# Two-stage convolution block on one core: a third buffer for half an image, loaded at another place and in quarters

## The chip, the core and the metric

The kernel runs on one core of a Trainium2 chip. The engines named here are TensorE (PE; PEld is its loading of weights), VectorE (DVE), ScalarE (ACT), GpSimd (POOL) and SyncE (SP), which issues all DMAs. The metric is the device time of one execution in microseconds.

## What is computed

`x` is (16, 32, 128, 128) in float32. Two residual steps follow each other:

```python
x = x + L0(_gn(x))      # per-image mixed 3x3 depthwise weights, gate, then 32 -> 32 channels
x = x + L1(_gn(x))
# L1:
hidden = einsum('oc,bchw->bohw', w_hidden, x)            # 32 -> 192 channels
hidden = depthwise 3x3(hidden)                           # SAME padding
q, k, v = split(hidden, 3)                               # 64 channels each
out = irfft2(rfft2(patches(q)) * rfft2(patches(k)))      # 8x8 patches
out_norm = layernorm over the 64 channels(out) * norm_w + norm_b
y = einsum('oc,bchw->bohw', w_out, v * out_norm)         # 64 -> 32 channels
```

`_gn` normalizes each channel over its image.

## The kernel before

The first stage handles image by image: `x` comes in, L0 is computed, and two things are written to memory: `x2_d` (the result of the first residual step, float32) and `xn_d` (the normalized input of L1, split in a high and a low float16 part, with a border of zeros). This takes some 500 us and the change hardly touches it.

The second stage runs over 32 units, each half an image (`u = 2 * image + half`). A unit has a *front* and a *spectral* stretch, and the front of unit u also finishes unit u-1 (its *tail*).

- **Front.** VectorE's `window` (copy L1107) copies one row of patches, 16 patches of 10 x 10 pixels, from the half image `xs` into a buffer `win`; there are 8 rows in a unit and four buffers. TensorE's `hidden_group` (matmuls L568) multiplies a quarter of a row at a time, 32 groups in a unit; ScalarE copies them to `hwin` (L815). Between the groups TensorE computes the v convolution of the tail from the tail's `xs` (`v_chunk`, L587), transposes its normalized pixels (`turn`, L600) and projects (`project`, L609). VectorE computes the tail's statistics (`pixel_stats` L1117, `variance` L1123 and L1125), centres and scales (`centre` L1130, `scale` L1137), gates (`gate` L1142) and adds the residual (`residual` L1149); GpSimd takes the roots (L451).
- **Spectral.** TensorE transforms eight octets of q (L648) and k (L662), VectorE multiplies them (L1201), TensorE goes back (`inverse`, L677, four times), ScalarE moves q (L857) and the result (L870). The last parts of the tail (turn, gate, project, residual) lie in its first third. Four window copies of the next unit stand between the products.

Each engine runs a list written out by hand; what orders them is semaphores. SyncE issues all DMAs. For unit u it waits until the tail's v convolution is done (`s_v_mm`, in `unit_dma`), loads the half image of unit u+1 in four DMAs (`load_xs`, L338: g is one of four copies over 32 partitions each, 536 KB), waits until the tail's four residuals are added, stores them (`store_res`, L391, 4 x 256 KB), waits for this store and loads `res` for unit u (`load_res`, L384, 4 x 256 KB from `x2_d`). There are two `xs` buffers: unit u+1 takes the place of the tail u-1, whose v convolution runs through the whole front of u.

The order in `unit_dma`:

```python
sp.wait_ge(s_v_mm, 8 * u)
if nxt is not None:
    load_xs(*nxt)
sp.wait_ge(s_res_done, 4 * u)
store_res(*prev)
sp.wait_ge(s_out_stored, 64 * u)
if here is not None:
    load_res(*here)
```

A program prints here the functions that the diff touches:

Of the kernel before, what the change touches and what calls it, by code (L numbers as in the profile page):

```python
# [68 lines left out]
def build(nc, t, out):  # L69
# [3 lines left out]
    x = t["x"]  # L73
# [18 lines left out]
    with ctx:  # L92
# [19 lines left out]
        s_xs_in = [semaphore(f"xs_in{s}") for s in range(2)]  # L112
# [128 lines left out]
        dw_t = take(128)  # L241
# [19 lines left out]
        ones_row = take(128)  # L261
        st1, st2 = take(6 * NCH), take(6 * NCH)
# [17 lines left out]
        res = take(2048)  # L280
        top[0] = max(top[0], stage1_end)
        xs = [take(HALF * WP, f16) for _ in range(2)]
        G_q = take(64 * 64)
        G_k = take(64 * 64)
        win = [take(1632, f16) for _ in range(4)]
# [21 lines left out]
        def _(sp):  # L307
# [43 lines left out]
            for b in range(-1, NB + 2):  # L351
# [10 lines left out]
                if b == NB + 1:  # L362
                    load_xs(0, 1)
# [3 lines left out]
                if b == NB - 3:  # L367

                    sp.wait_ge(s_xn_out, 128 * (older + 1))
                    sp.wait_ge(s_pads_stored, 32)  # L370
                    load_xs(0, 0)
# [8 lines left out]
            def load_res(b, half):  # L380
                for jr in range(2):
                    for s in range(2):
                        p0 = 64 * jr + 32 * s
                        sp.dma_start(res[p0:p0 + 32, :].rearrange("p (l r) -> p l r", l=2),  # L384
                                     image_rows(x2_d, b, half, jr, s)).then_inc(s_res_in, 16)

            def store_res(b, half):
                for jr in range(2):
                    for s in range(2):
                        p0 = 64 * jr + 32 * s  # L390
                        sp.dma_start(image_rows(out.rearrange("b c h w -> b c (h w)"), b, half, jr, s),  # L391
                                     res[p0:p0 + 32, :].rearrange("p (l r) -> p l r", l=2)).then_inc(s_out_stored, 16)
# [3 lines left out]

            def unit_dma(u, prev, here, nxt):

                sp.wait_ge(s_v_mm, 8 * u)
                if nxt is not None:  # L400
                    load_xs(*nxt)
                sp.wait_ge(s_res_done, 4 * u)
                store_res(*prev)
                sp.wait_ge(s_out_stored, 64 * u)
                if here is not None:
                    load_res(*here)

            for b in range(NB - 1):
                unit_dma(2 * b + 1, (b, 0), (b, 1), (b + 1, 0))
                unit_dma(2 * b + 2, (b, 1), (b + 1, 0), (b + 1, 1))  # L410
            unit_dma(LAST, (NB - 1, 0), (NB - 1, 1), None)
            unit_dma(LAST + 1, (NB - 1, 1), None, None)
# [4 lines left out]
        def _(pool):  # L417
# [11 lines left out]
            for s in range(4):  # L429
# [3 lines left out]
            pool.wait_ge(s_win_room, 4)  # L433
# [25 lines left out]
        def _(pe):  # L459
# [94 lines left out]
            def hidden_group(u, g, ring):  # L554
# [9 lines left out]
                w = win[g // 4 % 4]  # L564
# [7 lines left out]
            def v_chunk(u, half, k, jr, groups, between):  # L572
# [10 lines left out]
                for tap in range(9):  # L583
                    dy, dx = tap // 3, tap % 3
                    for s in range(2):
                        row = 8 * (2 * s + jr) + dy
                        mm = pe.matmul(v_banks[chunk % 3][64 * s:64 * s + 64, :], v_w[:, 64 * tap:64 * tap + 64],  # L587
                                       at(xs[half], row * WP + 32 * k + dx, [32 * WP, 2], [WP, 8], [1, 32]),
# [23 lines left out]
            def front(u, half, tail):  # L612
# [14 lines left out]
                v_half = 1 - half  # L627
                hidden(3)
                for k in range(4):
                    v_chunk(tail, v_half, k, 1, (5, 5, 4, 3)[k], hidden)  # L630
# [3 lines left out]
                    if k < 3:  # L634
                        v_chunk(tail, v_half, k + 1, 0, (5, 4, 3)[k], hidden)
# [3 lines left out]
            def spectral(u, half, tail):  # L639
# [57 lines left out]
                v_chunk(u, half, 0, 0, 0, None)  # L697

            front(0, 0, None)
            spectral(0, 0, None)  # L700
            for b in range(NB - 1):
                for half in (1, 0):
                    u = 2 * b + 2 - half
                    front(u, half, u - 1)
                    spectral(u, half, u - 1)
            front(LAST, 1, LAST - 1)
            spectral(LAST, 1, LAST - 1)
            front(None, 0, LAST)
# [179 lines left out]
        def _(dve):  # L888
# [212 lines left out]
            def window(u, half, r, b=None):  # L1101

                if positive(32 * u + 4 * (r - 3)):
                    dve.wait_ge(s_hidden_mm, 32 * u + 4 * (r - 3))
                if r == 0:
                    dve.wait_ge(s_xs_in[half], 64 * (b + 1))
                dve.tensor_copy(win[r % 4][:, 0:16 * WIN].rearrange("p (j y x) -> p j y x", y=10, x=10),  # L1107
                                     at(xs[half], 8 * r * WP, [8, 16], [WP, 10], [1, 10])).then_inc(s_win_ready, 1)
# [42 lines left out]
            def front(u, half, tail):  # L1151
                rows = iter(range(4, 8) if u is not None else ())

                def windows(n=1):
                    for r in islice(rows, n):
                        window(u, half, r)

                if tail is None:
# [6 lines left out]
                    windows(3)  # L1165
# [26 lines left out]
            def spectral(u, tail, nxt):  # L1192
# [74 lines left out]
```

## Time and profile before

| | us |
|---|---|
| median of 3 runs | 2653.68 (2650.85 to 2656.28) |
| profiled execution | 2649.98, its span 2648.2 |
| TensorE busy, over the span (48,375 matmuls, as many weight loads) | 2332.2 (88%) |
| VectorE busy | 1610.3 (61%) |
| ScalarE busy | 1453.6 (55%) |
| mean granted TensorE clock | 0.945 of full speed |

Times in the trace count from the span's start. The first unit's front starts at 501.6, unit 1's at 561.3, unit 11's at 1220.6, the last one's (unit 31) at 2548.1. A row of the timeline merges neighbouring instructions of one line; in square brackets stands the engine's idle time before it and what ended it. "issue" there means that the engine waited for nothing that the profile shows. Matmuls are pipelined, so the next group starts before the last one's modelled end.

### The profile page before, as it was taken

The numbers are of one execution on the slowest core, as the hardware profiler recorded it, in microseconds if no ns is written. First come the engines' busy times: TensorE is split into PE (matmuls) and PEld (weight loads), VectorE is DVE, ScalarE is ACT, GpSimd is POOL, SyncE is SP. The second block draws the span as 40 slices with busy tenths as digits, with TensorE's granted clock in tenths as the row PEclk, the third lists the DMA queues.
The fourth block names the chain that finished last, engine by engine and source line by source line (L and its number), as shares of the span: only waits on it lengthen the run. The fifth ranks groups of instructions, "written<-read, shape, count | busy, mean of one in ns | idle before, by whom it ended". The sixth has DMA issues, their size and how long they took to land. (4 is left out here: it accounts for less than half of the span.)

```text
span 2648.2 us, 107033 instructions
## 1 busy us (share of the span) xinstructions
PE 2332.2 (88%) x48375; PEld 1493.1 (56%) x48375; DVE 1610.3 (61%) x4058; ACT 1453.6 (55%) x2629; POOL 476.6 (18%) x324
## 2 busy tenths in 40 slices
PE   7898888698989889898998988989889899998997
PEld 3333333466656566565665666656666566665664
DVE  5667666466656566565665666656666556665565
ACT  3556555655555555555555555555555555555552
POOL 1000000022222222222222222222222222222222
PEclk9899889799999999999999999999999999999999
DMA  6788887723232232222322223222232222322222
GB/s 132 195 234 232 228 219 211 181 71 72 70 72 65 68 73 68 65 62 69 71 70 66 62 69 72 67 67 59 69 74 68 68 52 70 74 68 68 56 51 50
DMA packets 60409, 248.63 MB, mean 94 GB/s; under 512 B 12393, under 2 KB 12658, under 8 KB 53810
## 3 DMA queue, kind: packets, MB, share of 16 engines
q1 hardware_dynamic: 59954, 241.78, 38.0%
q8 instruction: 381, 6.24, 1.0%
q14 instruction: 74, 0.61, 0.1%
HBM read 140.02 MB, written 101.72 MB: 91 GB/s over the span
## 5 line engine op out<-in xcount | busy, mean ns | idle before, releaser
L451 POOL TENSOR_TENSOR arena<-arena 128x8 f32<-128x8 f32 x256 | 452.3, 1767 | 1666.1 <-DVE arena L1123 1661.1
L587 PE MATMUL bank<-arena 128*64 128x512 f16 x4608 | 689.8, 393 | 0.0
L815 ACT ACTIVATE arena<-bank 100x512 f32<-100x512 f32 x1024 | 605.2, 628 | 96.8 <-PE bank L568 75.6
L1201 DVE TENSOR_TENSOR arena<-bank,arena 128x512 f32<-128x512 f32 x512 | 334.7, 685 | 412.9 <-issue 322.8
L568 PEld LDWEIGHTS bank<-arena 128*36 128x36 f16 (+1 forms) x8192 | 330.9, 104 | 232.3 <-issue 25.1
L522 PE MATMUL bank<-arena 32*32 32x508 f32 (+1 forms) x9216 | 377.2, 637 | 50.1 <-issue 35.2
L568 PE MATMUL bank<-arena 128*36 128x128 f16 (+1 forms) x8192 | 389.9, 221 | 17.5 <-DVE arena L1107 9.6
L857 ACT ACTIVATE arena<-bank 128x512 f32<-128x512 f32 x256 | 153.2, 599 | 442.1 <-PE bank L648 440.1
L648 PE MATMUL bank<-arena 100*32 100x128 f32 x8192 | 311.2, 288 | 87.6 <-issue 85.9
L677 PE MATMUL bank<-arena 32*64 32x256 f32 x8192 | 303.0, 417 | 83.6 <-ACT arena L870 46.6
L662 PE MATMUL bank<-arena 100*32 100x128 f32 x8192 | 302.6, 285 | 36.7 <-issue 36.5
L870 ACT ACTIVATE arena<-bank 128x256 f32<-128x256 f32 x512 | 155.2, 390 | 319.2 <-PE bank L677 319.2
L1117 DVE BATCH_NORM_STATS2 arena<-arena 128x6 f32<-128x128 f32 x1024 | 221.7, 279 | 169.2 <-ACT arena L870 169.2
L824 ACT ACTIVATE arena<-bank,arena 128x256 f32<-128x256 f32 x512 | 261.5, 561 | 109.0 <-PE bank L600 108.6
L648 PEld LDWEIGHTS bank<-arena 100*32 100x32 f32 x8192 | 243.6, 115 | 110.7 <-issue 93.4
L662 PEld LDWEIGHTS bank<-arena 100*32 100x32 f32 x8192 | 238.1, 114 | 105.1 <-issue 81.6
L677 PEld LDWEIGHTS bank<-arena 32*64 32x64 f32 x8192 | 194.6, 143 | 166.4 <-issue 135.1
L1142 DVE TENSOR_TENSOR arena<-arena,bank 128x512 f32<-128x512 f32 x256 | 175.3, 685 | 149.4 <-ACT arena L824 149.2
L587 PEld LDWEIGHTS bank<-arena 128*64 128x64 f16 x4608 | 206.1, 109 | 96.1 <-issue 12.4
L522 PEld LDWEIGHTS bank<-arena 32*32 32x32 f32 x9216 | 143.1, 106 | 188.3 <-issue 155.7
L600 PEld LDWEIGHTS bank<-arena 128*128 128x128 f32 x1024 | 133.7, 195 | 107.9 <-DVE arena L1137 76.0
L1137 DVE TENSOR_TENSOR arena<-arena 128x512 f32<-128x512 f32 x256 | 178.1, 696 | 24.8 <-POOL arena L451 0.9
(112 smaller groups left out, 1615.6 us busy)
## 6 DMA issues: line engine op xcount, KB each, us to landing
arena<-xn_d SPq DMA_DIRECT2D x128, 536.2 KB, 8.4
xn_d<-arena SPq DMA_DIRECT2D x130, 260.0 KB, 4.8
x_d<-arena SPq DMA_DIRECT2D x64, 512.0 KB, 8.3
arena<-x_d SPq DMA_DIRECT2D x128, 256.0 KB, 5.0
out<-arena SPq DMA_DIRECT2D x128, 256.0 KB, 4.3
arena<-x_in SPq DMA_DIRECT2D x32, 544.0 KB, 9.8
arena<-x_in SPq DMA_DIRECT2D x32, 528.0 KB, 9.6
arena<-spectra_in SPq DMA_DIRECT2D x1, 384.0 KB
```

Source lines behind the costliest of these rows:

```text
L451: pool.tensor_tensor(tiny["rstd"][:, slot], tiny["var_eps"][:, slot], powers, ALU.pow).then_inc(s_root, 1)
L522: mm = pe.matmul(at(psum_of(t, r)[32 * c:32 * c + 32, :], low, [W, 4], [1, high - low]), conv_w[b % 2][32 * r:32 * r + 32, 32 * tap:32 * t ...
L568: mm = pe.matmul(ring[g % len(ring)][low:high, 128 * i:128 * i + 128], w[:, first + low:first + high], hidden_w, start=True, stop=True)
L587: mm = pe.matmul(v_banks[chunk % 3][64 * s:64 * s + 64, :], v_w[:, 64 * tap:64 * tap + 64], at(xs[half], row * WP + 32 * k + dx, [32 * WP, ...
L648: mm = pe.matmul(q_bank[32 * c:32 * c + 32, first:first + 128], G_q[0:WIN, 64 * ch + 32 * part:64 * ch + 32 * part + 32], hwin[0:WIN, 128 ...
L662: mm = pe.matmul(k_banks[m % 2][32 * c:32 * c + 32, first:first + 128], G_k[0:WIN, 64 * ch + 32 * part:64 * ch + 32 * part + 32], hwin[0:W ...
L677: mm = pe.matmul(i_banks[c][64 * lam:64 * lam + 64, 256 * (e % 2):256 * (e % 2) + 256], small["inverse"][32 * c:32 * c + 32, 64 * both:64 ...
L815: act.activation(h_rows[0:WIN, :, first:first + 4], ring[g % len(ring)][0:WIN, :].rearrange("p (i c) -> p c i", i=4), ACT.Copy).then_inc(s ...
L824: ins = act.activation(at(gated[jr], 256 * lam, [32, 8], [8, 4], [1, 8]), at(banks[4], 64 * lam, [8, 8], [128, 4], [1, 8]), ACT.Identity, ...
L1117: ins = dve.bn_stats(T["pixel_stats"][:, first:first + 6], at(Y, 2048 * s + 4 * p + j, [32, 64], [1, 2]))
L1137: dve.tensor_tensor(piece, piece, over(T["rstd"][:, slot]), ALU.mult).then_inc(s_y_norm, 1)
L1201: dve.tensor_tensor(prod[:, first:first + 512].rearrange("p (a b x) -> p a b x", a=2, b=2), at(k_banks[m % 2], 256 * quad, [128, 2], [0, 2 ...
```

## The change

- There are three `xs` buffers; unit u uses `xs[u % 3]`. The third lies where the first stage has its data, and the small `dw_t` moves among that data to make room.
- `load_xs` for unit u+1 is issued when the first hidden group of unit u is done (`s_hidden_mm` at 32u+1), and after each of its four DMAs SyncE waits for its landing before it issues the next. (The loads of units 0 and 1, in the first stage, stay without such waits.)
- `store_res` waits after each of its four DMAs.
- `load_res` is issued in two halves of two DMAs. The first waits for the third inverse product of unit u, the second for the first half's landing.
- There are three `win` buffers in place of four. Three rows are copied ahead of a unit (in the spectral stretch, after products 8, 10 and 12) in place of four (after 8, 10, 11 and 13); row 3 is now copied in the front, before the first `scale`. The copy of row r waits for 4(r-2) hidden groups of its unit in place of 4(r-3).
- The loops over image and half become one loop over u.

```diff
-            def load_xs(b, half):
+            def load_xs(u, paced=True):
+
+                b, half = divmod(u, 2)
                 for g in range(4):
                     src = xn_d[b, g % 2, :, half * (H // 2):half * (H // 2) + HALF, :].rearrange("c h w -> c (h w)")
-                    sp.dma_start(xs[half][32 * g:32 * g + 32, :], src).then_inc(s_xs_in[half], 16)
+                    sp.dma_start(xs[u % 3][32 * g:32 * g + 32, :], src).then_inc(s_xs_in[u % 3], 16)
+                    if paced:
+                        sp.wait_ge(s_xs_in[u % 3], 64 * (u // 3) + 16 * (g + 1))
...
+            def load_res(u, pair):
+                for s in range(2):
+                    p0 = 64 * pair + 32 * s
+                    sp.dma_start(res[p0:p0 + 32, :].rearrange("p (l r) -> p l r", l=2),
+                                 image_rows(x2_d, u // 2, u % 2, pair, s)).then_inc(s_res_in, 16)
+
+            def store_res(u):
+
+                y = out.rearrange("b c h w -> b c (h w)")
+                sp.wait_ge(s_res_done, 4 * (u + 1))
+                for part in range(4):
+                    pair, s = divmod(part, 2)
+                    sp.dma_start(image_rows(y, u // 2, u % 2, pair, s),
+                                 res[32 * part:32 * part + 32, :].rearrange("p (l r) -> p l r", l=2)).then_inc(s_out_stored, 16)
+                    sp.wait_ge(s_out_stored, 64 * u + 16 * (part + 1))
...
+            load_res(0, 1)
+            for u in range(1, LAST + 1):
+                if u < LAST:
+                    sp.wait_ge(s_hidden_mm, 32 * u + 1)
+                    load_xs(u + 1)
+                store_res(u - 1)
+                sp.wait_ge(s_inverse_mm, 4 * u + 3)
+                load_res(u, 0)
+                sp.wait_ge(s_res_in, 64 * u + 32)
+                load_res(u, 1)
+            store_res(LAST)
...
-                w = win[g // 4 % 4]
+                w = win[(8 * u + g // 4) % 3]
...
-            def window(u, half, r, b=None):
-
-                if positive(32 * u + 4 * (r - 3)):
-                    dve.wait_ge(s_hidden_mm, 32 * u + 4 * (r - 3))
+            def window(u, r):
+
+                if positive(32 * u + 4 * (r - 2)):
+                    dve.wait_ge(s_hidden_mm, 32 * u + 4 * (r - 2))
...
-            def front(u, half, tail):
-                rows = iter(range(4, 8) if u is not None else ())
+            def front(u, tail):
+                rows = iter(range(3, 8) if u is not None else ())
...
                     variance(tail, p)
                     if p == 1:
                         centre(tail, 0)
+                windows()
                 scale(tail, 0)
...
-                    if nxt is not None and n in (8, 10, 11, 13):
-                        window(nxt[0], nxt[1], (8, 10, 11, 13).index(n), nxt[2])
+                    if u < LAST and n in (8, 10, 12):
+                        window(u + 1, n // 2 - 4)
```

## Rows read from the trace of the kernel before

**Rows 1.** Windows, units 1 to 30 (the first line names the columns).

```profile
core 0: us, PE busy (x) PEld busy (x) DVE busy (x) ACT busy (x) POOL busy (x), PEclk, DMA share, GB/s
...
561.30:2548.10 1986.80, 1779.28 (x36482) 1225.34 (x36480) 1204.95 (x3002) 1093.75 (x2160) 424.82 (x240) 0.95 0.29 67
```

**Rows 2.** List of TensorE's waits, units 1 to 30: total us, times, longest us.

```profile
PE bank L648 <- issue: 82.5, 25, 5.4
PE bank L677 <- ACT arena L870: 43.7, 30, 1.5
PE bank L677 <- issue: 36.9, 23, 4.1
PE bank L662 <- issue: 34.3, 12, 4.3
```

**Rows 3.** Timeline of TensorE, unit 11: start us, us, engine, line, operation, count, idle before.

```profile
1253.76 1.06 PE L662 MATMUL bank<-arena 100*32 100x128 f32 x32
1254.66 0.41 PE L648 MATMUL bank<-arena 100*32 100x128 f32 x3
1257.66 1.07 PE L648 MATMUL bank<-arena 100*32 100x128 f32 x29 [2.60 <-issue]
...
1260.23 1.94 PE L662 MATMUL bank<-arena 100*32 100x128 f32 x32
1261.94 1.31 PE L648 MATMUL bank<-arena 100*32 100x128 f32 x32
```

**Rows 4.** Windows of unit 11, about the stall.

```profile
1244.60:1248.60 4.00, 4.00 (x60) 2.60 (x58) 2.98 (x6) 3.25 (x6) 0.00 (x0) 1.00 0.00 0
1248.60:1254.80 6.20, 6.01 (x147) 4.60 (x142) 3.30 (x6) 3.86 (x7) 0.00 (x0) 1.00 0.91 202
...
1257.60:1262.60 5.00, 4.94 (x81) 3.22 (x84) 1.00 (x2) 0.60 (x1) 0.00 (x0) 0.66 0.49 104
```

**Rows 5.** DMA queues: the page's q8, then the DMA view of 1240.9 to 1254.7.

```profile
q8 instruction: 381, 6.24, 1.0%
...
q1 hardware_dynamic: 96, 1.24, 40.4%
```

**Rows 6.** Timeline of SyncE, unit 11.

```profile
1248.48 1.82 SPq L338 DMA_DIRECT2D arena<-xn_d  x4
```

**Rows 7.** Timeline of unit 31: two DMA issues of SyncE, one group of TensorE.

```profile
2585.08 2.78 SPq L391 DMA_DIRECT2D out<-arena  x4
2591.39 2.19 SPq L384 DMA_DIRECT2D arena<-x_d  x4
...
2600.05 0.84 PE L662 MATMUL bank<-arena 100*32 100x128 f32 x17 [2.25 <-issue]
```

**Rows 8.** Timeline of TensorE: units 31 and 16, stretches without a stall.

```profile
2548.12 0.84 PE L568 MATMUL bank<-arena 128*64 128x128 f16 x24
...
2591.69 2.00 PE L677 MATMUL bank<-arena 32*64 32x256 f32 x64
...
1602.00 2.00 PE L677 MATMUL bank<-arena 32*64 32x256 f32 x64
...
1615.98 0.83 PE L568 MATMUL bank<-arena 128*64 128x128 f16 x24
```

**Rows 9.** Timeline, start of unit 11's front: VectorE, then TensorE's first turn.

```profile
1223.66 0.69 DVE L1137 TENSOR_TENSOR arena<-arena 128x512 f32<-128x512 f32 x1
...
1225.66 0.57 DVE L1107 COPY arena<-arena 128x1600 f16<-128x1600 f16 x1
...
1224.56 0.71 PE L600 MATMUL bank<-arena 128*128 128x128 f32 x4
```

**Rows 10.** Timeline of SyncE, the last store.

```profile
2641.69 2.78 SPq L391 DMA_DIRECT2D out<-arena  x4
```

**Rows 11.** DMA issues (page; then 0 to 30 us): count, KB each, us to landing.

```profile
arena<-xn_d SPq DMA_DIRECT2D x128, 536.2 KB, 8.4
...
out<-arena SPq DMA_DIRECT2D x128, 256.0 KB, 4.3
...
arena<-tables_in SPq DMA_DIRECT2D x1, 224.0 KB, 2.6
```

More of the change, by code:

```diff
@@ L111, in build @@
         s_transforms_in = semaphore("transforms_in")
-        s_xs_in = [semaphore(f"xs_in{s}") for s in range(2)]
+        s_xs_in = [semaphore(f"xs_in{s}") for s in range(3)]
         s_res_in = semaphore("res_in")
@@ L240, in build @@
         v_w = take(9 * 64, f16)
-        dw_t = take(128)
         powers = take(8)
@@ L261, in build @@
         ones_row = take(128)
+        dw_t = take(128)
         st1, st2 = take(6 * NCH), take(6 * NCH)
@@ L280, in build @@
         res = take(2048)
+        xs_late = take(HALF * WP, f16)
         top[0] = max(top[0], stage1_end)
-        xs = [take(HALF * WP, f16) for _ in range(2)]
+        xs = [take(HALF * WP, f16) for _ in range(2)] + [xs_late]
         G_q = take(64 * 64)
         G_k = take(64 * 64)
-        win = [take(1632, f16) for _ in range(4)]
+        win = [take(1632, f16) for _ in range(3)]
         block = ctx.enter_context(nc.Block())
@@ L362, in _ @@
                 if b == NB + 1:
-                    load_xs(0, 1)
+                    load_xs(1, paced=False)
                 if older is not None:
@@ L570, in hidden_group, with v_chunk @@
                 mm.then_inc(s_hidden_mm, 1)
-            def v_chunk(u, half, k, jr, groups, between):
+            def v_chunk(u, k, jr, groups, between):
                 chunk = 2 * k + jr
@@ L626, in front @@
                     return
-                v_half = 1 - half
                 hidden(3)
                 for k in range(4):
-                    v_chunk(tail, v_half, k, 1, (5, 5, 4, 3)[k], hidden)
+                    v_chunk(tail, k, 1, (5, 5, 4, 3)[k], hidden)
                     if k > 0:
@@ L634, in front, with spectral @@
                     if k < 3:
-                        v_chunk(tail, v_half, k + 1, 0, (5, 4, 3)[k], hidden)
+                        v_chunk(tail, k + 1, 0, (5, 4, 3)[k], hidden)
                     if k < 3 or u is None:
                         turn(tail, k, 1)
-            def spectral(u, half, tail):
+            def spectral(u, tail):
                 def q_octet(m):
@@ L696, in spectral @@
                 inverse(3)
[L697 to L708, printed above, removed]
+                v_chunk(u, 0, 0, 0, None)
+            front(0, None)
+            spectral(0, None)
+            for u in range(1, LAST + 1):
+                front(u, u - 1)
+                spectral(u, u - 1)
+            front(None, LAST)
             project(LAST, 3)
@@ L1149, in residual, with front @@
                 dve.tensor_tensor(piece, banks[6].rearrange("p (l r w) -> p l r w", l=2, r=8), piece, ALU.add).then_inc(s_res_done, 1)
-            def front(u, half, tail):
-                rows = iter(range(4, 8) if u is not None else ())
+            def front(u, tail):
+                rows = iter(range(3, 8) if u is not None else ())
                 def windows(n=1):
                     for r in islice(rows, n):
-                        window(u, half, r)
+                        window(u, r)
                 if tail is None:
@@ L1207, in spectral @@
                         residual(tail, 3)
-                    if nxt is not None and n in (8, 10, 11, 13):
-                        window(nxt[0], nxt[1], (8, 10, 11, 13).index(n), nxt[2])
-            dve.wait_ge(s_win_room, 4)
-            for r in range(4):
-                window(0, 0, r, 0)
-            front(0, 0, None)
-            spectral(0, None, (1, 1, 0))
-            for b in range(NB - 1):
-                for half in (1, 0):
-                    u = 2 * b + 2 - half
-                    front(u, half, u - 1)
-                    spectral(u, u - 1, (u + 1, 1 - half, b + 1))
-            front(LAST, 1, LAST - 1)
-            spectral(LAST, LAST - 1, None)
-            front(None, 0, LAST)
+                    if u < LAST and n in (8, 10, 12):
+                        window(u + 1, n // 2 - 4)
+            dve.wait_ge(s_win_room, 3)
+            for r in range(3):
+                window(0, r)
+            front(0, None)
+            spectral(0, None)
+            for u in range(1, LAST + 1):
+                front(u, u - 1)
+                spectral(u, u - 1)
+            front(None, LAST)
             residual(LAST, 3)
```

44 lines of the change are left out of this document (9 added, 35 removed).

## The prediction

> **What bounds the kernel now.** I read first where the time lies. The 30 middle units (1 to 30) take 1986.8 us of a span of 2648.2, 66.2 us each; TensorE is busy 1779.3 us of them, VectorE 1205, ScalarE 1094, and the DMA engines are at 0.29 [rows 1]. So the units are TensorE's, and what counts is the 207.5 us in which it is idle there. The list of TensorE's waits gives them: 153.7 us in 60 stalls on "issue", that is on nothing the profile shows as a releaser, 5.1 us a unit, and 43.7 us (1.5 a unit) on ScalarE before the last inverse product [rows 2].
>
> The timeline of unit 11 shows what an issue stall is. In the middle of one L648 group of 32 matmuls, which holds no wait at all, TensorE stops 2.60 us [rows 3]. The timeline of SyncE says which data: the next half image (4 x 536 KB) is issued at 1248.48, just where the spectral stretch begins [rows 6].
>
> Two counts of records show why it happens there. In the front TensorE takes 118 instructions in 4.0 us, a read every 8.6 us; in the spectral stretch one group of 64 takes 0.90 us from start to start, a read every 3.6 us [rows 3, 4]. The same burst can be hidden in the first and not in the second.
>
> Unit 31 is the control. It loads no half image, and its stretch runs without a stall to 2597.8, with 1 MB of store issued at 2585.08 in it; its one issue stall, 2.25 us, comes behind the 1 MB residual load of 2591.39 [rows 7]. So the half image makes the first stall of each unit, and the residual load a second, smaller one.
>
> **The change, part by part.**
>
> 1. *The half image moves to the front.* With three buffers the load of unit u+1 is issued at the first hidden group of u, one quarter at a time. Without stalls a unit takes: first hidden group to inverse(1) in unit 31, 2548.12 to 2591.69, 43.57 us; inverse(1) to the next unit's first group in unit 16, 1602.00 to 1615.98, 13.98 us, the ScalarE wait of 1.47 in it [rows 8]. Together 57.6 us against 66.2. The difference, 8.6, is 5.1 of issue stalls, and 3.5 of half clock and of pauses too small to be listed: the granted clock is 0.95 over the units, and at the half level an L662 group takes 1.71 us in place of 0.90 (start to start) [rows 1, 3].
> Cost in the front: the reads there are 8.6 us apart, and unit 11 went 13.8 us without one before it stopped, so a read may be several us late. A paced quarter is 536 KB, at the 202 GB/s of [rows 4] 2.7 us of queue. I take no stall there.
>
> 2. *Store by quarters, in the spectral stretch.* 256 KB in flight at a time, some 1.3 us of queue, in place of 1 MB behind 2.1 MB. The trace has no paced store. Bounds: nothing, as the unpaced megabyte in unit 31 cost nothing, to one stall of 2.25 us as behind the residual load [rows 7]. *Residual load in pairs after the third inverse*: 512 KB, 2.5 us of queue, at a place where TensorE waits 1.47 us for ScalarE anyway and then goes on to the slow front; bounds again 0 and 2.25. I take 0.5 us a unit for both, nearer to nothing, since each piece in flight is a half or a quarter of the only burst of these kinds that stalled.
>
> 3. *Three window buffers.* Row r's copy now waits until row r-3 has been multiplied, and the copy of row 3 moves from the spectral stretch to before the first scale() of the front. The waits are met: unit 11 copies row 4 at 1225.66, 1.1 us after the first turn, ahead of which TensorE has done the eight groups that row 4 now asks for; later rows have more room. But VectorE's queue pays for the copy, 0.57 us, and behind it stands scale(0), which ends at 1224.35, 0.21 us before the first turn (L600, 1224.56) that waits for it [rows 9]. TensorE is in order, so the turn and all behind it come 0.57 - 0.21 = 0.36, with the semaphore's way about 0.45 us later. Bounds 0 and 0.57. Taken from the spectral stretch the copy gives nothing back: VectorE is not what TensorE waits for there [rows 2].
>
> 4. *SyncE's queue.* It now blocks after each piece. What is queued behind a quarter is the next piece only; nobody but SyncE stands there. Pieces by the page: 224 KB lands in 2.6 us, 256 KB of store with three others about it in 4.3, 536 KB so in 8.4 [rows 11]. Upper bound of a unit's chain: 4 x 8.4 + 4 x 4.3 + 2 x 4.3 = 59.4 us. With nothing else in flight I expect 4.7, 3.0 and 4.5 for a pair: 18.8 + 12 + 4.5 = 35 us, inside the unit. The half image is needed by VectorE's first window copy late in the spectral stretch, over 20 us after it lands; the residual is needed at the first residual() of the next front, over 10 us after.
>
> 5. *Once only.* The last store is issued at 2641.69 and the span ends at 2648.2, 6.5 us later, some 0.5 of it the closing instructions [rows 10]; four in a row take 4 x 3.0 = 12, between 10.4 and 17.2: +6. In unit 31 the 2.25 us stall goes with about 1.7 of half clock behind it, against 0.45 + 0.5 new: -3. Unit 0, the first stage, dw_t's new place and one memset less: nothing, since all that moves there is what SyncE does behind the stage's end.
>
> Sum: a unit goes from 66.2 to 57.6 + 0.45 + 0.5 = 58.5, -7.7; 30 units -231; unit 31 -3; end +6: **-228 us**. The profiled execution took 2649.98 us (span 2648.2), 3.7 under the median of 2653.68. From the median: 2653.7 - 228 = **2426 us**.
>
> **A rule that speaks against it.** The rows say that a read of instructions is held up for many us by queued data [rows 5]. The Trainium skill, DMA: Bandwidth & Descriptors, section Queues, rings and completion order, says that each DMA engine takes turns between its queues packet by packet, so a read on its own queue would wait for one packet and not for the backlog; Runtime: NRT & Kernel Launch, section Instruction fetch mechanics, says that the next 16 KB block is fetched while the current one runs and that this is mostly hidden. By these the stalls are not the burst's, and the sum would be only items 3 and 5. The trace speaks against that (13.8 us without a read beside a full DMA, none of which happens in unit 31), so I keep it as a rival.
>
> **Rivals.**
> A. *The stalls are the stretch's own* (slower than before). TensorE takes a read every 3.6 us there, and the reads cannot keep up whatever else flows; the half image only coincides. For it: unit 31's stall ends 8.7 us after the residual load was issued, twice what a piece of that size takes to land [rows 7, 11]. Against it: the same stretch runs to 2597.8 without one. Then nothing of 8.6 returns: 31 x 0.45 + 6 = +20, **2674 us**. It decides once more than 8.0 of the 8.6 us stay. 5%.
> B. *Small pieces still starve the stretch.* Store quarters spread over 12 us, so three reads of instructions meet one each, and the pair of residual loads another; one 2.25 us stall with 1.7 us of half clock stays in each unit. 31 x (3.95 - 0.5) = +107, **2533 us**. For it: a megabyte alone did it in unit 31. Against: its store did not. 11%.
> C. *The paced chain does not fit*, the change does not do what it says: with pieces as slow as in the mixed bursts, 59.4 us and some 3 of issues between the waits set the unit, about 62.5 us; 30 x 4.0 = +120, **2546 us**. Against: those medians contain the queueing that pacing takes away. 2%.
> D. *Nothing moves* beyond 0.2%, by stalls that move with the load to the front: 2%.
>
> **Range and chances.** 2426 holds if the residual is near 0.5 us a unit. Without it and without the 0.45 it is 2397; with 2.5 in place of 0.5 and the end at its upper bound 2426 + 62 + 5 = 2493. Range 2400 to 2495, 80% with the forecast in it; B and C (13%) lie above, A and D (7%) too. A measurement of this kernel can tell about 0.2%: faster 0.93 (forecast, B, C), same 0.02, slower 0.05.
>
> **What the new profile would show.** Steps 1 and 2: TensorE's issue waits under 1 us a unit and a granted clock of 1.00 in the units; q8 reads at even distances in the spectral stretch; DMA busy in the first 20 us of a unit. An issue stall beside the store or the pair of residual loads is B; stalls without DMA are A. Step 3: L600 waiting some 0.4 us for L1137 once a unit, no wait of the window copies for L568. Step 4: SyncE waits for hidden groups and for residual(), so it has time to spare. Step 5: the end 6 us later after the last residual(). The prediction is wrong if the units' mean is above 60.5 us.

## The result, and the profile after

| | before | changed |
|---|---|---|
| median, us | 2653.16 (2650.85 to 2656.28) | 2413.9 (2407.77 to 2421.74) |
| ratio, 95% interval | 1 | 0.9099 (0.9069 to 0.9130) |
| profiled execution, us | 2649.98 | 2421.74, its span 2419.6 |
| predicted | | 2426 (2400 to 2495) |

The windows by stage answer to [rows 1]. The columns are the same; unit 1 begins at 571.1 here and the last unit at 2319.8.

```profile
core 0: us, PE busy (x) PEld busy (x) DVE busy (x) ACT busy (x) POOL busy (x), PEclk, DMA share, GB/s
0.00:571.10 571.10, 478.65 (x10506) 218.18 (x10508) 341.19 (x889) 314.13 (x381) 24.23 (x67) 0.89 0.79 195
571.10:2319.80 1748.70, 1687.82 (x36484) 1177.02 (x36482) 1208.35 (x3002) 1095.67 (x2160) 434.28 (x240) 1.00 0.34 76
2319.80:2419.60 99.80, 82.51 (x1392) 51.28 (x1388) 64.43 (x170) 44.67 (x88) 27.83 (x16) 0.96 0.17 39
```

The 30 middle units went from 1986.8 to 1748.7 us, 66.2 to 58.3 each: -238.1, which is the whole of the -239 between the medians. TensorE's idle time in them fell from 207.5 to 60.9 us (146.6), and the other 91.5 us come out of its busy time, which fell from 1779.3 to 1687.8 for the same records: the granted clock is 1.00 where it was 0.95. The waits that the profile lists for these units before the change sum to 207.2 us, so nearly all idle time is listed, and what no list shows is the longer busy time at the half level. The last stage took 99.8 us where it took 100.1. All that comes before unit 1 took 571.1 us here and 561.3 before, though the change hardly touches it; in the experiments below unit 1 begins between 561.1 and 571.9 without system, so this is taken as the spread from run to run. These 9.8 us are the difference between the 238 us of the units and the 228 us by which the two profiled executions differ.

TensorE's list of waits over the same units answers to [rows 2] (total us, times, longest us):

```profile
PE bank L677 <- ACT arena L866: 43.7, 30, 1.5
PE bank L601 <- DVE arena L1133: 8.8, 29, 0.3
PE bank L601 <- ACT arena L820: 5.8, 30, 0.2
PE bank L677 <- issue: 1.0, 2, 0.7
PE bank L677 <- DVE arena L1198: 0.7, 1, 0.7
PE bank L648 <- issue: 0.5, 2, 0.3
```

The issue stalls were 157.7 us (153.7 in [rows 2], and one of 4.0 us at L609 that those rows leave out) and are 1.5 us. The wait for ScalarE stands as it was, 43.7 us. New is a wait of the turn (L601) for the scale (L1133), 0.3 us in 29 of 30 units.

Where the transfers lie now is on SyncE's timeline of unit 11, which begins at 1155.9 and whose spectral stretch begins at 1185.7 (start, length until the last issue):

```profile
1156.33 15.77 SPq L341 DMA_DIRECT2D arena<-xn_d  x4
1193.18 8.33 SPq L397 DMA_DIRECT2D out<-arena  x4
1208.45 5.68 SPq L388 DMA_DIRECT2D arena<-x_d  x4
```

Half image in the front, store in the middle of the stretch, residual load behind the third inverse. In the stretch's 12 us of store the DMA view has three reads of instructions beside the 1.05 MB of data, a read every 4 us, where [rows 5] had none in 13.8:

```profile
q1 hardware_dynamic: 320, 1.05, 39.9%
q8 instruction: 3, 0.05, 1.5%
```

And the DMA issues of the units, which answer to [rows 11] (count, KB each, us to landing): every piece lands sooner than before, now that at most one other piece is queued with it.

```profile
arena<-xn_d SPq DMA_DIRECT2D x120, 536.2 KB, 4.8
out<-arena SPq DMA_DIRECT2D x120, 256.0 KB, 2.7
arena<-x_d SPq DMA_DIRECT2D x120, 256.0 KB, 4.2
```

### The profile page after: what moved, and what is told of

Same layout as the page of the kernel before. It is cut to its first block, busy times and chain, and to the rows that moved or that the text cites. A ratio compares the mean times of both kernels' runs of the same rounds, so it can differ in the third digit from the quotient of the medians.

```text
span 2419.6 us, 107091 instructions
## 1 busy us (share of the span) xinstructions
PE 2249.0 (93%) x48375; PEld 1446.5 (60%) x48375; DVE 1614.0 (67%) x4058; ACT 1454.5 (60%) x2629; POOL 486.3 (20%) x323
## 4 chain that ended last, share of the span: by engine, by line
PE 83%; DVE 7%; ACT 6%; issue 3%; DMA 1%; SPq 0%; POOL 0%; ACTq 0%; POOLq 0%
PE bank L588 17%; PE bank L523 16%; PE bank L677 11%; PE bank L662 10%; PE bank L648 8%; PE bank L601 7%; PE bank L569 7%; PE bank L610 5%; DVE arena L1113 3%; ACT arena L866 3%; DVE arena L1133 1%; ACT arena L820 1%; DVE arena L1126 1%; DVE arena L1103 1%; ACT arena L725 1%
## 5 line engine op out<-in xcount | busy, mean ns | idle before, releaser
L452 POOL TENSOR_TENSOR arena<-arena 128x8 f32<-128x8 f32 x256 | 462.1, 1805 | 1413.9 <-DVE arena L1119 1408.9
L523 PE MATMUL bank<-arena 32*32 32x508 f32 (+1 forms) x9216 | 386.4, 657 | 49.9 <-issue 35.1
L677 PE MATMUL bank<-arena 32*64 32x256 f32 x8192 | 264.8, 386 | 48.8 <-ACT arena L866 46.6
L648 PE MATMUL bank<-arena 100*32 100x128 f32 x8192 | 277.6, 274 | 4.3 <-issue 2.9
L662 PE MATMUL bank<-arena 100*32 100x128 f32 x8192 | 277.1, 274 | 0.1
L662 PEld LDWEIGHTS bank<-arena 100*32 100x32 f32 x8192 | 221.0, 109 | 54.7 <-issue 25.6
L677 PEld LDWEIGHTS bank<-arena 32*64 32x64 f32 x8192 | 180.7, 131 | 107.6 <-issue 78.2
L648 PEld LDWEIGHTS bank<-arena 100*32 100x32 f32 x8192 | 220.7, 109 | 20.5 <-issue 4.1
L601 PEld LDWEIGHTS bank<-arena 128*128 128x128 f32 x1024 | 133.6, 195 | 119.5 <-DVE arena L1133 88.7
L601 PE MATMUL bank<-arena 128*128 128x128 f32 x1024 | 181.4, 300 | 18.1 <-DVE arena L1133 10.8
```

Of the source, the lines that this page charges most:

```text
L452: pool.tensor_tensor(tiny["rstd"][:, slot], tiny["var_eps"][:, slot], powers, ALU.pow).then_inc(s_root, 1)
L523: mm = pe.matmul(at(psum_of(t, r)[32 * c:32 * c + 32, :], low, [W, 4], [1, high - low]), conv_w[b % 2][32 * r:32 * r + 32, 32 * tap:32 * t ...
L601: tr = pe.transpose(t_bank[:, 128 * i:128 * i + 128], at(Y, 8 * k + 4 * jr + i, [32, 128]), ident)
L648: mm = pe.matmul(q_bank[32 * c:32 * c + 32, first:first + 128], G_q[0:WIN, 64 * ch + 32 * part:64 * ch + 32 * part + 32], hwin[0:WIN, 128 ...
L662: mm = pe.matmul(k_banks[m % 2][32 * c:32 * c + 32, first:first + 128], G_k[0:WIN, 64 * ch + 32 * part:64 * ch + 32 * part + 32], hwin[0:W ...
L677: mm = pe.matmul(i_banks[c][64 * lam:64 * lam + 64, 256 * (e % 2):256 * (e % 2) + 256], small["inverse"][32 * c:32 * c + 32, 64 * both:64 ...
```

## The experiments

Theory: a read of TensorE's instructions waits behind the bytes that are queued on the DMA engines, and TensorE stops when it has used up what it holds; so the length of the queue and the pace at which instructions are used decide. Rivals: the pacing alone, the earlier arrival through the third buffer alone, the kernel's own waits, and the turn-taking of the DMA engines packet by packet. All kernels but one start from the changed one; each is compared with the kernel before, whose median was 2646, 2654 or 2652 us beside them and 2653 beside the changed kernel; so differences between medians below are uncertain by some 10 us. For each kernel the windows of units 1 to 30 are shown: us, then TensorE's busy time; the three columns at the end are granted clock, DMA share and GB/s.

### Where the half image is loaded, and whether it is paced

**All four quarters at once, in the front.**

```diff
-                    load_xs(u + 1)
+                    load_xs(u + 1, paced=False)
```

> The changed kernel, but the four quarters of the half image are issued in the front all at once. Theory (a read of instructions waits behind the data queued; in the front it may be many us late): the 2.1 MB are some 10 us of queue, TensorE takes a read every 8.6 us there; at most a short stall where a read falls early in the burst, 0 to 1 us a unit: 2414 to 2445 us, nearest to 2420. Rival (the pacing is what removed the stalls, not the place): one stall of 3 to 4 us a unit with half clock behind it, 2550 us or more.

Measured: 2419.78 us, ratio 0.916 (0.9129 to 0.9192). The units are 58.5 us each:

```profile
561.50:2315.25 1753.75, 1686.98 (x36486) 1177.40 (x36484) 1208.38 (x3001) 1096.05 (x2160) 434.29 (x240) 1.00 0.34 76
```

Issue stalls sum to 8.3 us in 30 units, the longest 2.2, and the clock stays up. In the front 2.1 MB of queue is nearly free. Pacing brings 0.2 us a unit by the two profiles; the medians differ by 6 us and the ratios by 16 us, with intervals that just overlap, so its size is not settled.

**At the old place, all at once.** The load is that of unit u+2, so that no engine waits for it sooner.

```diff
-                if u < LAST:
-                    sp.wait_ge(s_hidden_mm, 32 * u + 1)
-                    load_xs(u + 1)
+                if u == 1:
+                    sp.wait_ge(s_hidden_mm, 33)
+                    load_xs(2)
+                if u + 2 <= LAST:
+                    sp.wait_ge(s_v_mm, 8 * u)
+                    load_xs(u + 2, paced=False)
```

> The changed kernel, but the half image is issued at the old place, when the tail's v convolution is done, all four quarters at once; what is loaded is the half image of unit u+2, so nobody waits for it sooner. All else as changed. Theory: the first stall of each unit comes back, 3 to 4 us with 1.7 to 3.4 us of half clock behind it: 29 units x 5.5 = +160, 2575 us (2550 to 2610). Rival (the gain came from the earlier arrival of the half image, or from the store and residual load alone): 2414 to 2430 us.

Measured: 2590.39 us, 0.9802 (0.9765 to 0.9840), 176 more than the changed kernel. The stalls are back, 112.1 us on issue (first row the windows, then from the list of waits; lines are shifted by three):

```profile
563.40:2480.66 1917.26, 1746.07 (x36484) 1206.39 (x36482) 1208.31 (x3001) 1095.64 (x2160) 434.33 (x240) 0.97 0.31 70
```

```profile
PE bank L651 <- issue: 60.0, 15, 6.1
PE bank L665 <- issue: 24.2, 7, 4.3
PE bank L680 <- issue: 22.8, 7, 4.1
PE bank L613 <- issue: 5.1, 1, 5.1
```

This kernel has the third buffer and pacing of all else; the place of the half image is old, and its four quarters go at once. The trace also shows how much TensorE holds. Between a read that landed at 1224.5 and the stall at 1238.7 no other read lands, and two windows of it give

```profile
1224.55:1238.70 14.15, 13.94 (x239) 9.12 (x236) 9.21 (x20) 9.62 (x17) 1.64 (x1) 1.00 0.45 97
1238.70:1241.40 2.70, 0.00 (x0) 0.00 (x0) 1.19 (x2) 0.00 (x0) 0.00 (x0) 0.85 1.00 203
```

475 instructions in 14.15 us, then none: a little under two reads of 254.

How such a stall ends can be read directly. In unit 11 of the kernel before, the DMA view has no read of instructions from 1240.9 to 1254.8; one starts between 1254.8 and 1254.9 and is through at 1256.15, and TensorE goes on at 1257.66 [rows 3]. The data of the half image on either side of that read are (1240.9 to 1254.8, then 1254.9 to 1261.1)

```profile
q1 hardware_dynamic: 99, 1.25, 40.7%
q1 hardware_dynamic: 86, 0.89, 69.8%
```

So the read came when 1.25 MB of the burst had started, with 0.89 MB still to come: it was held up by a large part of the queue, not by all of it. Every other stall ends in the same way. Take units 1 to 30 of the kernel before, of the changed one and of the ten kernels in this section and the next two: TensorE has 241 pauses of over 0.6 us there, the ScalarE wait before an inverse product left out, and each ends 1.2 to 1.7 us after a read of instructions has landed.

**At the old place, paced.** The same with `paced=True`.

> As the kernel with the late load of unit u+2, but each quarter waits for the one before. Theory by queue length: a read meets at most 2.7 us of queue in a stretch that needs one every 3.6 us; short stalls, seldom with half clock: 0.5 to 2 us a unit, 2430 to 2475 us. Rival (the place alone decides): as the unpaced late load, 2575 us. Rival (the pacing alone decides): 2414 us.

Measured: 2443.62 us, 0.9249 (0.9224 to 0.9274), 30 more than the changed kernel. 18.4 us of issue stalls in 32 pieces, at most 2.0, and the clock up:

```profile
561.10:2338.85 1777.75, 1699.89 (x36484) 1180.84 (x36482) 1208.55 (x3001) 1095.44 (x2160) 434.31 (x240) 1.00 0.32 75
```

So of the 176 us that the burst costs at the old place, pacing alone saves 147 and the place alone 171. Each is nearly enough by itself; the rivals by which only the one or only the other counts both fall.

### The store and the residual load

**Both as before**, the store at once and the load at once behind it.

```diff
-                    sp.wait_ge(s_out_stored, 64 * u + 16 * (part + 1))
+                sp.wait_ge(s_out_stored, 64 * (u + 1))
...
-                sp.wait_ge(s_inverse_mm, 4 * u + 3)
                 load_res(u, 0)
-                sp.wait_ge(s_res_in, 64 * u + 32)
                 load_res(u, 1)
```

> The changed kernel with the store of the tail unpaced and the residual load issued right behind it, four pieces at once, as before the change. Theory: the second stall of each unit comes back, 1 to 2.3 us, now and then with half clock: +1.2 to +2.5 us a unit, 2450 to 2490 us. Rival (only the half image mattered): 2410 to 2418 us.

Measured: 2507.79 us, 0.9474 (0.9440 to 0.9507), 94 more, and above the range of 2450 to 2490 that was expected.

```profile
571.90:2421.00 1849.10, 1728.98 (x36482) 1195.75 (x36480) 1208.46 (x3002) 1096.94 (x2160) 434.52 (x240) 0.98 0.31 72
```

59.7 us are issue stalls, 2.0 a unit, as expected (1 to 2.3); what the expectation had too low is the time at half clock (0.98 over the units, with 41 us more of TensorE's busy time than in the changed kernel, 1.4 a unit). The timeline of one unit has both stalls, the small one from the store (issued at 1285.26) and the large one from the load (1291.70):

```profile
1293.44 1.57 PE L675 MATMUL bank<-arena 32*64 32x256 f32 x48 [0.88 <-issue]
...
1300.21 0.77 PE L660 MATMUL bank<-arena 100*32 100x128 f32 x16 [2.87 <-issue]
```

The reads of instructions tell the two apart. No read starts while the data of the store move, from 1286.1 to 1291.1, and one starts at 1291.2; none starts from 1292.2 to 1297.6 beside the residual load, and one does at 1297.6. TensorE goes on 2.3 and 2.6 us after these starts. The data that went ahead, by the DMA views of 1284.3 to 1291.1 and of 1292.2 to 1297.6, were

```profile
q1 hardware_dynamic: 319, 1.05, 65.3%
q1 hardware_dynamic: 311, 1.04, 84.7%
```

Here nearly the whole megabyte went ahead of the read both times. The same view settles the stall of unit 31 that [rows 7] show: a read starts at 2597.2, just as the residual load is through (its last data end at 2597.8), and TensorE goes on at 2600.05.

In most units of the kernel before the second stall was shorter, about 1.2 us, though it reached 3.7. There TensorE is often at half clock, and so slow in using instructions, when the residual comes; that this is the reason was not tried.

**The store alone at once**, the load late and in pairs.

> The changed kernel with the four pieces of the store issued at once; the residual load stays late and in pairs. Theory: 1 MB of queue gives the short stalls seen beside the store in the kernel with both as before, 0.3 to 0.9 us in half of the units: +5 to +20 us, 2420 to 2434 us. Rival (the store was most of what that kernel lost): 2460 us or more.

Measured: 2421.99 us, 0.914 (0.9107 to 0.9172), 8 more than the changed kernel; the two intervals overlap. 6.8 us of issue stalls in 15 pieces.

```profile
563.10:2319.26 1756.15, 1690.64 (x36484) 1178.33 (x36482) 1208.40 (x3001) 1096.05 (x2160) 434.36 (x240) 1.00 0.33 76
```

So what that part of the change gives lies nearly all in the load, its place and its halves together, and not in the paced store. Place and halves of this load were not tried apart.

**Only this part, on the kernel before.** Store by pieces and load in pairs behind the third inverse; two half image buffers, four window buffers.

```diff
                         sp.dma_start(image_rows(out.rearrange("b c h w -> b c (h w)"), b, half, jr, s),
                                      res[p0:p0 + 32, :].rearrange("p (l r) -> p l r", l=2)).then_inc(s_out_stored, 16)
+                        sp.wait_ge(s_out_stored, 64 * (2 * b + half) + 16 * (2 * jr + s + 1))
...
                 if here is not None:
+                    sp.wait_ge(s_inverse_mm, 4 * u + 3)
                     load_res(*here)
```

(and a wait on `s_res_in` between the pairs)

> The kernel before with one part of the change alone: the store by single pieces, the residual load in pairs after the third inverse product. Half image, two buffers and four window buffers as before. Theory: the second stall of each unit goes, the first stays: as the changed kernel with the late unpaced load (2590 us) or a little under it, 2570 to 2600 us. Rival (third buffer and earlier arrival matter by themselves): over 2620 us.

Measured: 2584.34 us, 0.9758 (0.9722 to 0.9794). The units are 64.0 us, as in the kernel with the late load:

```profile
569.40:2490.00 1920.60, 1751.71 (x36484) 1208.34 (x36482) 1204.04 (x3001) 1093.00 (x2160) 424.70 (x240) 0.96 0.31 70
```

So the third buffer and the other windows bring nothing by themselves; the kernel with the late load is even 6 us slower (12 by the ratios), and it has the wait of the turn for the scale, 9.2 us in 30 units, that this one lacks. Added to the kernel before, the residual part alone gives 68 us (2652 to 2584) and the half image's part alone 138 (2646 to 2508, the kernel with store and load both as before); taken from the changed kernel they cost 94 and 176. The sums are 206 and 270, the whole change is 239: the two parts act on each other. That one stall changes where the next burst falls would do this; no run shows it.

### The traffic by itself

Here each spectral stretch gets a load that nobody needs: into the buffer that is free then, to be loaded again before use. The load is some quarters of the half image at once.

```diff
+            def extra(u):
+
+                b, half = divmod(u, 2)
+                for g in range(1):
+                    src = xn_d[b, g % 2, :, half * (H // 2):half * (H // 2) + HALF, :].rearrange("c h w -> c (h w)")
+                    sp.dma_start(xs[u % 3][32 * g:32 * g + 32, :], src).then_inc(s_extra, 16)
...
                 if u < LAST:
+                    if u > 1:
+                        sp.wait_ge(s_extra, 16 * (u - 1))
                     sp.wait_ge(s_hidden_mm, 32 * u + 1)
                     load_xs(u + 1)
+                if u + 2 <= LAST:
+                    sp.wait_ge(s_v_mm, 8 * u)
+                    extra(u + 2)
                 store_res(u - 1)
```

(as for one quarter; `range(2)` and `range(4)` with waits for 32 and 64 in the next two. SyncE alone waits for this load, at the start of the next unit, and in the trace with four quarters it never stood there.)

**One quarter.**

> The changed kernel, plus at the start of each spectral stretch one quarter of a half image (536 KB) loaded into the buffer that is free then; it is loaded again later, so it is traffic that nobody needs or waits for. Theory (a read of instructions waits behind what is queued): some 2.5 us of queue against a read every 3.6 us, at most 0.3 us a unit: 2410 to 2425 us. Rival (it is not the traffic): 2414 us here and in the three others of this set.

**Two.**

> The same with two quarters at once, some 5 us of queue. Theory: stalls of 0 to 2.5 us by where a read falls in it, some with half clock: +0.7 to +2 us a unit, 2435 to 2475 us. Rival (it is not the traffic): 2414 us.

**Four.**

> The same with four quarters at once, 2.1 MB in packets of 17 KB, some 10 us of queue. Theory: stalls as with the half image at its old place, though no wait of any engine depends on this traffic: 2570 to 2605 us. Rival (the stall came from the kernel's own waits on the half image): 2414 us.

**Four, in packets of 4 KB.** The source is `x2_d`, 512 KB a DMA in rows of 4 KB. A packet here is what the profile counts as one: a row of the transfer.

> The same 2.1 MB at once, taken from the first stage's result in packets of 4 KB in place of 17 KB. If a read of instructions waits for all bytes queued before it, nothing changes: 2570 to 2605 us. If the DMA engines take turns between queues packet by packet and it waits for one or a few packets, the stall shrinks to a quarter: 2414 to 2450 us.

| at the start of the stretch | us | ratio (95%) | us a unit |
|---|---|---|---|
| nothing (the changed kernel) | 2413.9 | 0.9099 (0.9069 to 0.9130) | 58.3 |
| 0.5 MB | 2407.12 | 0.9089 (0.9050 to 0.9127) | 58.0 |
| 1.1 MB | 2449.78 | 0.9243 (0.9204 to 0.9281) | 59.3 |
| 2.1 MB | 2591.48 | 0.9775 (0.9716 to 0.9834) | 64.2 |
| 2.0 MB in 4 KB packets | 2583.05 | 0.9750 (0.9693 to 0.9807) | 63.8 |

The windows of the four, in this order:

```profile
563.00:2304.15 1741.15, 1682.06 (x36484) 1174.93 (x36482) 1208.26 (x3001) 1096.23 (x2160) 434.29 (x240) 1.00 0.37 86
```

```profile
563.50:2341.16 1777.65, 1698.15 (x36484) 1180.58 (x36482) 1208.46 (x3002) 1096.23 (x2160) 434.35 (x240) 1.00 0.41 93
```

```profile
570.80:2496.96 1926.16, 1753.96 (x36486) 1209.46 (x36484) 1208.56 (x3002) 1096.75 (x2160) 434.53 (x240) 0.96 0.46 102
```

```profile
567.20:2482.66 1915.46, 1747.80 (x36486) 1205.67 (x36484) 1208.40 (x3002) 1096.91 (x2160) 434.49 (x240) 0.96 0.45 101
```

Half a megabyte costs nothing (2407 us, 3 under the range expected), one costs 1.2 us a unit more than that, two cost 6. The first of the four moves more data than the changed kernel (share 0.37 against 0.34) and is not slower: it is not the amount that counts but what is queued at once. And packets a quarter as long change next to nothing. The issue waits of the last kernel are those of the one with full packets (113.2 us there):

```profile
PE bank L661 <- issue: 59.2, 15, 5.6
PE bank L675 <- issue: 26.0, 10, 4.6
PE bank L690 <- issue: 18.8, 7, 3.7
PE bank L623 <- issue: 4.8, 1, 4.8
```

If a read of instructions waited for one row of the data, the stall would have shrunk with the row. So it is not rows that count but bytes. How many of the queued bytes go ahead of a read, this doesn't tell: it was nearly all of 1.05 MB above, and 1.25 MB of a half image. The rule weighed in the prediction (the Trainium skill, DMA: Bandwidth & Descriptors, section Queues, rings and completion order) lets the engines take turns between queues by packets, but its packet is a group of typically 9 to 17 descriptors. Turns row by row are excluded here; turns by groups of that size are not.

### Two further versions

**Row 3 behind the first scale.**

```diff
-                windows()
                 scale(tail, 0)
+                windows()
                 centre(tail, 1)
```

> The changed kernel with one line moved: VectorE copies window row 3 behind the first scale of the front in place of before it. Theory (the three-buffer schedule costs TensorE 0.31 us a unit at the first turn, as the profile of the changed kernel has it): that wait goes and 31 x 0.31 = 9.6 us with it, 2404 us (2398 to 2410). Rival (the copy's 0.57 us costs the same further down VectorE's queue): 2414 us.

Measured: 2401.18 us, 0.9069 (0.9036 to 0.9103).

```profile
563.40:2296.76 1733.36, 1683.37 (x36485) 1177.49 (x36482) 1208.33 (x3001) 1096.56 (x2160) 439.27 (x240) 1.00 0.34 77
```

Its interval overlaps that of the changed kernel, so the medians alone don't settle the 9.6 us expected; the list of waits does. Of the 60.5 us in the changed kernel's list these 49.7 are left:

```profile
PE bank L677 <- ACT arena L866: 43.7, 30, 1.5
PE bank L601 <- ACT arena L820: 5.8, 30, 0.2
PE bank L588 <- issue: 0.2, 1, 0.2
```

The wait for the scale is gone and nothing has taken its place.

**The last inverse product in other banks.** What remains is the 43.7 us before the fourth inverse product: it waits until ScalarE has copied the third out of the same four PSUM banks. Banks 0, 1, 6 and 2 are idle then. This kernel also has row 3 behind the first scale, as above, and issues the last unit's store at once.

```diff
-        i_banks = [banks[3], banks[5], banks[7], banks[4]]
+        i_banks = [[banks[3], banks[5], banks[7], banks[4]]] * 3 + [[banks[0], banks[1], banks[6], banks[2]]]
+        i_order = [(0, 1, 2, 3)] * 3 + [(3, 1, 0, 2)]
...
-                if g in (1, 2) and positive(16 * u):
-                    pe.wait_ge(s_y_ready, 16 * u - (3, 1)[g - 1])
+                if g == 0 and positive(16 * u):
+                    pe.wait_ge(s_y_ready, 16 * u - 2)
...
                 if chunk == 0:
-                    pe.wait_ge(s_prod_ready, 16 * (u + 1))
-                if chunk == 1:
-                    pe.wait_ge(s_y_ready, 16 * (u + 1) - 2)
+                    pe.wait_ge(s_y_ready, 16 * (u + 1) - 3)
                 if chunk == 2:
-                    pe.wait_ge(s_q_copied, 8 * (u + 1))
+                    pe.wait_ge(s_y_ready, 16 * (u + 1))
...
-                    if positive(16 * u + 4 * e):
+                    if positive(16 * u + 4 * e) and e < 3:
                         pe.wait_ge(s_y_ready, 16 * u + 4 * e)
...
-                for c in range(4):
+                for c in i_order[e]:
```

> Row 3 behind the first scale, the last unit's store issued at once, and the last inverse product of a unit written to four PSUM banks that are idle then, so that it need not wait until ScalarE has copied the one before; the first part of the v convolution, in one of these banks, waits for ScalarE's first copy in its place. Theory: of the 1.47 us wait per unit some 0.6 stays at the v convolution, and the last store gives back 4 us: 2414 - 31 x 1.2 - 4 = 2373 us (2362 to 2385). Rival (the products of the last octet or the first scale come too late, and the wait only moves): 2400 to 2410 us.

Measured: 2367.47 us, 0.8938 (0.8905 to 0.8971), 46 us under the changed kernel and the fastest of all. Against the kernel with row 3 behind the scale alone it is 34 us: 27 in the 30 units (1733.4 to 1706.3), which is the banks' share, 0.9 a unit, and 6 in the last stage, where the store at once helps too. The wait has become 0.5 us at the v convolution, on ScalarE's first copy:

```profile
565.50:2271.76 1706.26, 1682.85 (x36486) 1179.56 (x36483) 1208.62 (x3002) 1095.04 (x2160) 439.26 (x241) 1.00 0.34 78
```

```profile
PE bank L588 <- ACT arena L866: 15.7, 30, 0.6
```

TensorE is now busy 1682.9 of 1706.3 us in the units.

## Why the prediction was right

- **The bound and the cause.** That the issue stalls are missing instructions, held up by queued data, was read from one window without a q8 row and one unit without a half image. The loads that nobody needs show it directly: stalls follow the bytes queued at once, though no computing engine waits for them. That each stall ends 1.2 to 1.7 us after a read has landed shows what TensorE stood for. Rival A (the stretch's own pace) falls: in the changed kernel the stretch runs at the full pace with reads every 4 us and 1.5 us of issue stalls in 30 units. What was taken as speaking for it, the stall of unit 31 that ends 8.7 us after the residual load was issued, fits the queue too: its read landed at 2598.6, behind the load's data.
- **The rule that spoke against it.** The prediction took one packet to be little beside the backlog, and so found the rule at odds with the traces. By the Trainium skill (DMA: Bandwidth & Descriptors, section Queues, rings and completion order) a packet is typically 9 to 17 descriptors; if a row is one descriptor, a half image, 128 rows over 16 DMA engines, gives each engine 8, no more than one such packet (an estimate). So the rule, read with its own size, need not speak against the cause.
- **Item 1, 57.6 us from two stretches without a stall.** Held: cut where VectorE begins the tail's statistics, 11 of the 30 units take 57.9 us and none less, and 57.9 less the 0.3 at the turn is 57.6. The two pieces, taken from units 31 and 16, were a better guide than the sum of listed stalls (5.1 of the 8.6 us), since the half clock doesn't stand in any list. The prediction's "pauses too small to be listed" were not there to find: the listed waits are 207.2 of the 207.5 us of idle time, and the rest of the loss lay in the busy time. That the front takes a paced quarter for nothing held, and it takes all four for almost nothing.
- **Item 2, 0.5 us for the pieces in the stretch.** As stalls too high; 1.5 us of issue stalls in 30 units is 0.05 a unit. The mean unit, 58.3, is yet 0.4 above 57.6 + 0.3: two units of 30 fell to half clock and took 60.5 us, which is 0.2 of it, and the rest stands in TensorE's busy time without a cause that the profile shows. That the total comes near the 0.5 is in part luck. Rival B, at 2533 us, would have needed more in one piece: 1.1 MB extra at the start of a stretch cost 1.2 us a unit, and no piece of the changed kernel is over half of that.
- **Item 3, 0.45 us at the first turn.** The mechanism held to the line (L601 waits for L1133, once a unit), the size was 0.30. In unit 11 the scale ended 0.48 us later against the unit's first hidden group, not 0.57: the copy is 0.57 long, but the next instruction starts 0.49 after it. And from the scale's end to the turn it takes 0.06 here, not 0.09. So 0.48 less the 0.21 of room, with 0.06, is 0.33, which is how much later the turn starts.
- **Item 4.** 4.8, 2.7 and for a pair of residual loads about 4.5 us, against 4.7, 3.0 and 4.5. By its list of waits SyncE stands 614.5 us in the units before the store, until the last residual is added (L394 <- L1145), 20 a unit, so rival C is out.
- **Item 5.** The last store takes 11.0 us from its issue (2408.63) to the end, against 6.5: +4.5 in place of +6. Unit 31 and its tail up to that store took 88.8 us against 93.6: -4.8 in place of -3.
- **The sum.** Units -238 for -231, the last stage -0.3 for +3: -239 for -228. The 11 us are those two: the prices of items 2 and 3 were 0.1 and 0.15 us a unit too high, some 7 us together, and that of item 5 was 3 us too high. That the profiled executions differ by just 228 is the spread before unit 1 and no support.

## What to carry to other kernels

A stall of TensorE that no semaphore explains, beside full DMA engines, is likely its own instruction stream: look for the gap in the instruction queue's reads, and count the instructions per us of each stretch. Then check that each stall ends just after such a read lands. Put bulk transfers where TensorE uses few instructions per us (few and long matmuls). Elsewhere keep less queued than moves in the time in which TensorE uses up one read of instructions: here TensorE uses up a read in 3.6 us of the stretch; 0.5 MB, which moves in 2.7 us, was free, and 1.1 MB, 5.3 us, was not. A semaphore wait behind each piece, in the queue of an engine that has time to spare, does it. For the floor, add up stretches that ran without a stall rather than subtract the listed stalls: here over a third of the gain, 91 of 238 us, was busy time, longer at half clock above all, which stands in no list of waits.

## What the runs showed of the hardware

- TensorE held 475 instructions after a read had landed, then stopped: a little under two reads of 254. Over all stalls with the half image's or a whole extra burst at the stretch's start it was 469 to 532. At the spectral pace (64 in 0.90 us) 475 last less than 7 us, at the front's pace (118 in 4.0 us) some 16.
- All 241 stalls of over 0.6 us for instructions, in twelve kernels, ended 1.2 to 1.7 us after a 16 KB read had landed. A read did not always wait for all data queued: 1.25 of 2.14 MB went ahead of it in one burst, 1.04 of 1.05 MB in another.
- In the stretch 0.5 MB queued at once cost nothing, 1.1 MB 1.2 us a unit and 2.1 MB 6 us; in the front 2.1 MB cost 0.2. The length of the rows, 17 or 4 KB, made no difference.
- The clock followed: 0.95 to 0.97 over the units in the kernels with a stall of some 2 to 6 us in nearly every unit, 0.98 with stalls of 1 to 3 us in most (store and residual load as before), 1.00 in all others, though TensorE also stops 1.47 us in each unit in all of them but the last.
